# A macaron block (FFN, gated slot attention, FFN) on one core: three phases run into one another instead of standing apart, on one plan of PSUM banks, with weights prepared as they come into use

## What is computed

```python
q = swish(x @ Wq); k = swish(x @ Wk); v = x @ Wv
f = log_sigmoid(x @ Wf) / 8; s = 1 - exp(f)
for t in range(T):                      # two running states
    hk = hk * exp(f[t]) + outer(k[t], s[t])
    p = softmax((q[t] * K ** -0.5) @ hk)
    hv = hv * exp(f[t])[:, None] + outer(s[t], v[t])
    o[t] = p @ hv
out = (o * rsqrt(mean(o * o) + eps) * g).reshape(...) @ Wo
```

## Time and profile before

| | |
|---|---|
| median of 3 executions | 3148.86 us (3148.39 to 3149.68) |
| the profiled execution | 3146.56 us |
| its span, first to last instruction | 3144.8 us |
| PE busy | 2997.2 us, 95% |
| DVE busy | 2616.9 us, 83% |
| ACT busy | 1410.8 us, 45% |
| POOL busy | 1253.1 us, 40% |
| granted clock of PE | 0.99 of 2.4 GHz |

### The profile page before, as it was taken

The page is one execution under the profiler, slowest core; times in us unless marked ns, Lnnn a source line. Parts: engine busy times, 40 slices in busy tenths (PEclk is TensorE's granted clock), DMA queues, the critical chain, the costliest instruction groups (busy, mean ns, idle before and its releaser), DMA issues. The chain is left out here.

```text
span 3144.8 us, 97450 instructions
## 1 busy us (share of the span) xinstructions
PE 2997.2 (95%) x34688; PEld 2616.9 (83%) x34688; DVE 2616.9 (83%) x4369; ACT 1410.8 (45%) x4042; POOL 1253.1 (40%) x2170
## 2 busy tenths in 40 slices
PE   4999999999999999699999999999699999999999
PEld 3888888888888888588888888888588888888888
DVE  6888888888888887388888888888699999999998
ACT  2333333333333333577777777777222222222222
POOL 3333333333333333255555555555333333333332
PEclk9999999999999999899999999999799999999999
DMA  4444434433444443344444444444222222222222
GB/s 96 115 126 122 122 122 128 123 121 121 128 124 122 122 122 116 107 128 129 128 131 126 129 130 130 126 130 124 70 80 75 73 78 74 74 78 74 75 78 58
DMA packets 485055, 340.86 MB, mean 108 GB/s; under 512 B 301940, under 2 KB 451828, under 8 KB 484984
## 3 DMA queue, kind: packets, MB, share of 16 engines
q1 hardware_dynamic: 276088, 289.53, 29.3%
q10 hardware_dynamic: 208896, 50.38, 8.1%
HBM read 155.19 MB, written 117.44 MB: 87 GB/s over the span
## 5 line engine op out<-in xcount | busy, mean ns | idle before, releaser
L633 PE MATMUL mid_ps<-ffn_xT_hl,w_hl 128*128 128x128 f16 x12288 | 729.3, 219 | 0.0
L432 PE MATMUL res_bank<-w_hl,midT_hl 128*128 128x256 f16 x6144 | 712.6, 273 | 6.3 <-DVE low_hl L580 5.7
L633 PEld LDWEIGHTS mid_ps<-ffn_xT_hl,w_hl 128*128 128x128 f16 x12288 | 703.8, 98 | 3.9 <-issue 0.6
L513 ACT ACTIVATE midT_hl<-mid_ps 128x1024 f16<-128x1024 f32 x256 | 261.9, 1023 | 922.0 <-PE mid_ps L644 917.6
L432 PEld LDWEIGHTS res_bank<-w_hl,midT_hl 128*128 128x128 f16 x6144 | 595.0, 98 | 75.9 <-DVE midT_hl L574 8.8
L390 POOL TENSOR_TENSOR ffn_var_eps<-ffn_moments,eps_col 128x1 f32<-128x1 f32 x256 | 94.0, 367 | 1297.9 <-DVE ffn_moments L386 1297.9
L553 DVE TENSOR_TENSOR_SCAN runmax<-restart,logits_ps 128x1024 f32<-128x1024 f32 x256 | 585.4, 2287 | 9.1 <-PE logits_ps L622 1.3
L574 DVE SCALAR_TENSOR_TENSOR midT_hl<-mid_ps,midT_hl 128x1024 f16<-128x1024 f32 x256 | 312.5, 1221 | 192.9 <-ACT midT_hl L513 192.9
L558 DVE TENSOR_TENSOR step<-runmax 128x1024 bf16<-128x1024 f32 x256 | 314.5, 1229 | 8.9
L432 PE MATMUL qkvf_ps<-wqkfv_hl,att_xT_hl 128*128 128x512 f16 (+1 forms) x1536 | 291.5, 326 | 3.1 <-DMA att_xT_hl<-att_xn_hl 1.6
L406 ACT ACTIVATE ffn_xn_hl<-ffn_xc,ffn_rstd 128x256 f16<-128x256 f32 x256 | 129.7, 507 | 313.9 <-POOL ffn_xc L397 286.6
(11 more groups left out here) (144 smaller groups left out, 5818.5 us busy)
## 6 DMA issues: line engine op xcount, KB each, us to landing
projected<-qkvf_out SPq DMA_DIRECT2D x128, 512.0 KB, 2.7
qkv<-projected SPq DMA_DIRECT2D x128, 384.0 KB, 3.4
x<-x_out SPq DMA_DIRECT2D x256, 128.0 KB, 1.8
x_res<-x SPq DMA_DIRECT2D x256, 128.0 KB, 2.2
x_in<-in_L_attn_x SPq DMA_DIRECT2D x128, 128.0 KB, 2.1
x_res<-in_L_attn_x SPq DMA_DIRECT2D x128, 128.0 KB, 2.1
gate<-projected SPq DMA_DIRECT2D x128, 128.0 KB, 3.1
x_in<-x SPq DMA_DIRECT2D x128, 128.0 KB, 2.1
```

The source lines that it names most:

```text
L432: last = nc.tensor.matmul(dst, left(lp, k), right(rp, k), start=(k == 0 and lp == rp), stop=(k == blocks - 1 and lp == 1))
L513: nc.scalar.activation(midT_hl[:, t.slot, 0], mid_ps[t.slot][:, :], ACT.Relu).then_inc(mid_high_made, 1)
L633: nc.tensor.matmul(mid_ps[t.slot][:, cols], w1_hl[:, wp, k, cols], xT_hl[:, t.ring, xp, k], start=(c % PER_BANK == 0 and k == 0 and wp == xp),
```

## The change

**One Block.** `pipeline` becomes a class `Phase` with a place in time, `starts_at`, and a function `flow` that writes all three phases of an engine into one program. The draining steps of one phase are merged, by a global step number, with the filling steps of the next; at equal numbers the drain goes first. Attention starts at step 131, the second FFN at 262. The barriers and the waits for all stores are gone: `begin` on SP waits for the stores of the first 32 tiles only.

```diff
+        self.loop_to = self.loop_from + self.trips * unroll
+
+    def step(self, s, i=None):
+        if s == self.first and self.opening:
+            self.opening()
+        for stage, offset, extra in self.stages:
+            if i is not None or 0 <= s + offset < self.tiles + extra:
+                stage(Tile(self.base + s + offset, self.base, self.tiles, i, self.unroll))
+        if s == self.end - 1 and self.closing:
...
+
+    draining = []
+    for phase in phases:
+        filling = [(phase.starts_at + s, 1, phase, s) for s in range(phase.first, phase.loop_from)]
+        for _, _, which, s in sorted(draining + filling, key=lambda e: e[:2]):
+            which.step(s)
+        with eng.Fori(0, phase.trips) as i:
+            for s in range(phase.unroll):
+                phase.step(phase.loop_from + s, i)
+        draining = [(phase.starts_at + s, 0, phase, s) for s in range(phase.loop_to, phase.end)]
+    for _, _, which, s in draining:
+        which.step(s)
 
 
 def build(nc, a, out, tiles, d_model, d_ff, d2, d_low, heads):
@@ -134,11 +149,11 @@
```

```diff
-            bank_T = psum(scope, "bank_T", BANK)
-            bank_state = psum(scope, "bank_state", BANK)
-            bank_G = psum(scope, "bank_G", BANK)
-            bank_o = psum(scope, "bank_o", BANK)
-            bank_ends = psum(scope, "bank_ends", BANK)
...
+            bank_G, bank_T, bank_state, bank_pair = bank(0), bank(1), bank(2), bank(3, 2)
...
+            bank_logits, bank_PtT, bank_o = bank(5), bank(6), bank(7)
...
-            o_ps = bank_o[:, 0:D]
-            out_ps, PtT_ps = bank_ends[:, 0:D], bank_ends[:, D:2 * D]
+            o_ps, out_ps = bank_o[:, 0:D], bank_o[:, D:2 * D]
+            PtT_ps = bank_PtT[:, 0:D]
```

```diff
+                def read_out(t):
+                    if is_first(t):
+                        pe.wait_ge(swish_made, tiles)
+
+                    pe.wait_ge(S["AB_masked"], t.n + 3)
+
+                    after(pe, S["o_raw_made"], t, lag=1)
+                    after(pe, S["att_res_added"], t, lag=4)
+                    with_state(t, o_ps, PtT[:, t.slot], 1, S["Hv_made"], masked[:, t.slot, :, 1],
+                               qkv[:, t.ring, 2], S["o_done"])
...
+                return Phase([(divide_o, -2), (decay_Hv, 0), (sum_squares, -2), (scale_logits, 0),
+                               (gate_logsig, 4), (mask_AB, 1, 2), (finish, -5), (add_states, 0), (decay_Hk, 1), (o_low, -2),
+                               (invert_totals, 0), (make_St, 2)],
...
+                def project_out(t):
...
+                    after_ring_dma(pe, oT_turned, t)
...
+                    after(pe, S["o_raw_made"], t, lag=-3)
+                    after(pe, S["att_res_added"], t, lag=1)
...
+                def transpose_Pt(t):
+                    after(pe, S["Pt_made"], t)
+
+                    after(pe, S["PtT_made"], t, lag=1)
...
+                return Phase([(transpose_kSt, 1), (logits, 0), (products_A, 1),
+                              (products_B, -1), (project_out, -5), (update_states, 0), (log_gate_sums, 2),
+                              (read_out, -1), (transpose_Pt, 0)],
...
+                return Phase([(load_residual, -4), (load_qkv, 2), (load_gate, 6), (store, -5), (turn_o, -3)],
+                             tiles, base, UNROLL, LONGEST_LAG, starts_at, begin, finish_stores)
```

```diff
+                def swish(t):
+                    if is_late(t, ROWS_BESIDE_ATTENTION - 1):
                         nc.scalar.preload_act_table_set("silu_and_others")
...
+                    after(act, qk_projected, t)
+                    nc.scalar.activation(qkvf_out[:, t.slot, 0:2], qkvf_ps[:, :].rearrange("p (n d) -> p n d", n=2),
+                                         ACT.Silu, scale=1.0 / S_ATT).then_inc(swish_made, 1)
+                    if is_late(t, ROWS_BESIDE_ATTENTION):
+                        nc.scalar.preload_act_table_set("natural_log_exp_and_others")
```

**Transposes on SP.** The two `turn` transfers of the FFNs are issued by SP instead of ACT. **Weights as needed.** The preparation stands in the fill of the first FFN, as stages that act for the first tile only. SP issues x's first load as its third transfer. Of DVE's list:

```diff
+                    stages = [(lambda t: norm.load(sp, t, src_t), 6), (first_only(load_up, sp), 5),
+                              (load_residual, 0), (store, -2),
+                              (lambda t: norm.turn(sp, t, mid_picked), 3), (first_only(load_down, sp), 3),
+                              (first_only(load_attention, sp), 2),
+                              (lambda t: norm2.turn(sp, t, qk_projected), -4), (store_projected, -6)]
...
+                    stages = [(finish, -2), (lambda t: norm.stats(dve, t), 5),
+                              (lambda t: norm2.stats(dve, t, out_made), -2), (low_of_x1, -3),
+                              (lambda t: norm.aggregate(dve, t), 5), (lambda t: norm2.aggregate(dve, t), -2),
+                              (first_only(rest_of_low_rank_in, dve), 5), (first_only(first_parts_of_bias, dve), 5),
+                              (lambda t: norm.low(dve, t), 4), (first_only(rest_of_low_rank_out, dve), 4),
+                              (first_only(rest_of_up, dve), 3), (mid_low, 0), (low_low, 2), (first_max, 1),
+                              (reached, 1), (reject, 1), (first_only(rest_of_down, dve), 1),
+                              (first_only(scale_out_weights, dve), 0), (first_only(rest_of_attention, dve), -2)]
```

1515 lines of the change are left out of this document (780 added, 735 removed).

## The result

| | before | after |
|---|---|---|
| median | 3148.80 us (3148.39 to 3149.68) | 3078.63 us (3076.98 to 3080.66, 4 executions) |
| profiled execution | 3146.56 us | 3076.98 us |
| its span | 3144.8 us | 3075.2 us |

The ratio is 0.9777, 95% interval 0.9765 to 0.979.

A forecast was written before the change was run, and what follows sets the result against it. PE was taken to bound both FFNs, no engine being full in attention; start -11.5, transitions -10 and -14, second FFN -1 and attention's loop 0 gave -36.5, so 3110.1 us profiled, 3112 as median, range 3090 to 3135.

The forecast's parts named there:

- Attention's loop: Three edits of order in attention's steps were to balance to 0 us, with -15 and +20 as bounds.
- (1): In attention, transpose_Pt no longer waits for finish; 35 us in 128 steps if on the chain, which the trace spoke against.
- (2): In attention, project_out ahead of update_states, some 0.7 us, lets DVE's add_states start later in three steps of four.
- (3): In attention, read_out waits for this step's finish, behind DVE's masking, holding PE about 0.3 us in chunk 3.
- Rival (b): Attention's loop gains: most of the removed wait's 35 us is real, about 3080 us; chance 0.10.
- Rival (a): Attention's loop loses: the new orders cost 0.5 to 0.7 us in four steps, +16 to +23, 3131 us; chance 0.17.
- Rival (c): First transition: ACT's table loads cost 2.31 us each, +11.3, some hidden, 3121 us; chance 0.07.
- (d): SP's queue becomes the bound in the FFNs: transposes 0.3 us late in 256 steps, +77, 3190 us; chance 0.04.
- (e): No overlap at the phase changes: bank waits hold the fill until the drain ends, about 3147 us; chance 0.04.
- The start: Before the first FFN: first scan at 25 us, 16 earlier, less 4.5 for weight rests: -11.5, bounds -8 and -17.
- The first transition: First FFN to attention: interleaving gains 14.2 us on ACT, less 4 charged for PE's clock: -10, bounds -15 and -2.
- The second: -14 forecast: Attention to second FFN: first logits run 14.9 us earlier among the last output projections: -14, bounds -18 and -9.

The follow-up runs named there:

- after_Pt_waits: The changed kernel with the transpose of the probabilities waiting again, for DVE's reciprocal of this step directly ahead of the slots; 3080.13 us, ratio 0.9784.
- pe_order_alone: The kernel before with only PE's output projection moved ahead of the state update, DVE's finish at its old place and the old banks; 3161.84 us, ratio 1.0037.
- loop_alone: The kernel before, barriers kept, with only the attention loop changed: new order of stages, transposed probabilities in their own bank; 3123.38 us, ratio 0.9919.
- gate_low_moved: The kernel before with POOL's gate low part moved to the start of the next step, PE's waits unchanged; 3145.75 us, ratio 0.9988.
- gate_low_small: The kernel before with POOL making only the first of 256 columns of the gate's low part, the rest zero; 3132.87 us, ratio 0.9954.
- more_table_loads: The changed kernel with twelve more function table loads on ACT, two behind each of the six late swish instructions; 3100.85 us, ratio 0.9854.

## Why the prediction was wrong

The direction was right and the range was not: 3078.6 against 3090 to 3135.

**Attention's loop: 0 forecast, 24.7 us gained.** This is the step that failed. The 0 was the balance of +10 us of costs and an equal part of the 35 us of the removed wait, (1). The earlier trace rows had been read rightly, that the wait was off the chain: after_Pt_waits puts one back, even later, and nothing returns (3080.1 for 3078.6). So that part of the 35 us was nothing. The walk for (2) and (3) was mis-sized in all its terms. It gave +0.3, +0.3 and +0.1 us for three of the four chunks' steps and set "-0.1 to -0.2 in three" against it for the instruction of POOL that the decay then misses. That last term was the largest of all: L1025 lost 360 ns, not 100 to 200, because an instruction that meets POOL's is held to its end: the 0.73 and 0.91 us of L1025 in the trace before, against the 0.42 of a lone one, would have said so, and 0.36 in three steps of four is -0.27 a step, -1.08 in four. The slots give 0.3 of it back, which the walk did not have. Of the costs none is left against the kernel before. `read_out` does wait 0.3 us in chunk 3, as priced, but the transposes behind it come 0.39 us after the slots there, and came 0.42 after them before. The delay of `add_states` by PE's order costs something only where DVE has nothing in its stead (pe_order_alone); `finish` fills it. So +0.3 in four steps was -0.86 (4 x 0.214). The prediction's own sign of being wrong, a step more than 0.15 us off 7.14, shows it: it is 0.21 off. The bound of -15 was also too near: it had been set for the wait and not for the contention.

**Rival (b), 3080, was right in its number and wrong in its cause.** It said that the removed wait is worth most of 35 us; a wait put back costs 1.5 us between medians whose executions overlap. The measured 24.7 us in the loop and 8 us more than forecast in the other places happen to add up to the same time; that is luck. Rival (a) put the loop's sign wrong. Rival (c), dearer table loads, falls: 1245.48 to 1246.77 us in the changed kernel is one load and the next instruction.

```profile
1245.48 1.28 ACT L576 ACT_TABLE_LOAD   x1
1246.77 0.42 ACT L942 ACTIVATE absgate<-gate 128x256 f32<-128x256 f32 x1
...
1250.19 1.28 ACT L571 ACT_TABLE_LOAD   x1
1251.77 0.60 ACT L573 ACTIVATE qkvf_out<-banks 128x512 f32<-128x512 f32 x1 [0.29 <-PE banks L472]
```

The load's successor starts 0.01 us behind its end, so nothing here puts the 1.03 us of the earlier trace rows down to the load, and the transfer is left. The Trainium skill (ScalarE: Activation LUTs, What ACT_TABLE_LOAD costs) counts a drain with each switch, 2.66 us together; here no drain follows, neither between two loads nor ahead of an instruction that has its data. The second load, at 1250.19, lies in the wait for the projection as forecast, of which 0.29 us stay (0.31 were counted). Rivals (d) and (e) fall with the steps of 9.565 and 6.945 us, which did not change, and with the overlap's 10.5 and 15.1 us.

**The start: -11.5 forecast, 14.7 gained** (10.8 to 14.7, as said above, so the 3 us above the forecast are within what the start differs by). The first scan was to come at 25 us and came at 23.44: 

```profile
11.36 1.26 SPq L323 DMA_DIRECT2D w_f<-in_L_ffn_w  x2
...
19.11 1.91 ACT L401 ACTIVATE w_hl<-w_f 128x2048 f16<-128x2048 f32 x1 [0.42 <-DMA w_f<-in_L_ffn_w]
...
23.44 2.29 DVE L601 TENSOR_TENSOR_SCAN runmax<-restart,banks 128x1024 f32<-128x1024 f32 x1 [0.77 <-PE banks L680]
```

The down weights, issued at 11.36, were there at 19.1, 7.7 us later, where 20.5 to 22.4 was taken from the 10.4 of the earlier trace rows. Of the lead, 2.9 us were lost again by tile 8, where 4.5 were charged for the weights' rests on DVE; in the four traces with the lower clock it is 4.6 to 6.7.

**The first transition: -10 forecast, 12.7 gained,** of which 1.3 are the loop's own gain in its first nine tiles (loop_alone has it too, 1367.35 for 1368.63). The other 11.4 lie between the 14.2 that the sum for ACT gave and the 10 that were left with the charge of 4 us for PE's clock. The mean granted clock over these 80 us was 0.94, with 0.81 in 1260 to 1280.

**The second: -14 forecast, 16.5 gained.** The first logits ran at 2174.61, between the output projections as foretold, 11.3 us behind the transpose of tile 127 instead of 27.3, which is 16.0 for the 14.9 of the prediction:

```profile
2171.48 0.80 PE L472 MATMUL banks<-ffn_xT_hl,m_hl 128*128 128x128 f16 x6
...
2174.61 0.38 PE L678 MATMUL banks<-m_high,low_hl 128*128 128x512 f16 x1 [1.05 <-DVE low_hl L628]
```

**The second FFN: -1 forecast, 1.2 gained; the first: 0 forecast, 0.1 lost.**

## What to carry to other kernels

Cut a step of a software pipeline at the instructions on which the engines meet, and compare the segments: a wait that has gone from the list is no gain if its segment keeps its length. Where two engines hold each other up, as DVE and POOL do here, an edit of the order that only swaps instructions can be worth more than the wait it removes; compare the mean duration of each instruction in the loop with the shortest one of the same form, and lay the other engine's instructions beside waits or beside instructions that read PSUM. And an idle engine isn't free: an unused instruction on POOL cost 63 us here.

## What the runs showed of the hardware

DVE and POOL take turns, in most pairs. A DVE instruction of 128x256 elements with both inputs in SBUF takes 390 to 430 ns alone. Issued 0.2 us or more ahead of the end of a POOL instruction of 128x256 elements (0.67 to 0.73 us), it ends 0.28 to 0.29 us after POOL's, whatever its start, and so takes up to 0.94 (the slots in gate_low_moved), and 0.95 beside a POOL instruction that was held itself. One of 128x128 (L1036 in gate_low_moved) ends 0.15 us after POOL's. The instruction of POOL that comes second is held in the same way (0.93 for some 0.7). Those of DVE with an input in PSUM (`finish` 415 ns, `add_states` 682) kept their time to 30 ns with POOL beside them. 791 ns, the mean of L1025 before, was therefore nearly half wait (it takes 426 in gate_low_small). The exception is `logsig`: both inputs in SBUF, issued in all 101 steps beside POOL's `o_rms` of 128x4 elements and 1.01 us, it takes 0.43 us.

The Trainium skill (SBUF — State Buffer, Who interferes with whom) has it as a rule: a DVE instruction with two inputs in SBUF contends with a GpSimd instruction that reads SBUF, because its second input comes through an interface that the two engines share; the first to issue keeps the shared ports for its whole length; with at most one input in SBUF, outside DVE's two-port modes, there is no contention. The traces agree with it in all pairs named but the last: `o_rms` reads SBUF too, if only 4 elements wide, and doesn't hold `logsig`.

A load of ACT's function table is 1.28 us between starts 1.29 us apart, with no further cost wherever the next instruction has its data, in the traces of the changed kernel and of more_table_loads. The clock of PE over the 80 us of the first transition was 0.94 in the changed kernel and 0.79 where ACT kept it waiting for two more loads a step.
